# GpSimd's jump over the general path, the list building, the low halves and four weight loads, each moved within the rows' stage of a graph layer kernel

## The reference

```python
deg = jnp.maximum(jax.ops.segment_sum(jnp.ones(dst.shape), dst, 6250), 1.0)
xn = _layernorm(x)
# gnn: mean over the incoming edges, two linear layers
agg = jax.ops.segment_sum(xn[src], dst, 6250)
gnn = xn @ W1.T + b1 + (agg / deg[:, None]) @ W2.T + b2
# mix: linear attention, 16 heads of 32, relu on q and k
vk = einsum('bnhc,bnhd->bhcd', v_pad, k); vk_q = einsum('bnhd,bhcd->bnhc', q, vk)
mix = (vk_q[..., :-1] / (vk_q[..., -1:] + 1e-15)) @ proj_weight.T + proj_bias
x = x + gnn + mix
# ffn on layernorm(x): attention pooling -> gates -> two best of 8 experts, gelu, gelu
x = x + ffn(_layernorm(x))
```

## Time and profile before

| | us |
|---|---|
| three runs | 1461.55, 1464.06, 1466.59; median 1464.06 |
| the profiled execution | 1465.09 |
| its span, first to last instruction | 1462.9 |
| mean granted clock of TensorE | 0.977 of full |
| busy: PE / DVE / POOL / ACT | 1372.7 / 940.4 / 834.0 / 610.3 |

### The profile page before, as it was taken

The page is one execution under the profiler, slowest core; times in us unless marked ns, Lnnn a source line. Parts: engine busy times, 40 slices in busy tenths (PEclk is TensorE's granted clock), DMA queues, the critical chain, the costliest instruction groups (busy, mean ns, idle before and its releaser), DMA issues.

```text
span 1462.9 us, 22936 instructions
## 1 busy us (share of the span) xinstructions
PE 1372.7 (94%) x7764; PEld 625.1 (43%) x7764; DVE 940.4 (64%) x2087; ACT 610.3 (42%) x938; POOL 834.0 (57%) x907
## 2 busy tenths in 40 slices
PE   7888989999999999999999999899996889999997
PEld 3444434444444444444444444344442344444443
DVE  8877343222566877777777767666764466776677
ACT  5645223232233444444434444333332436555554
POOL 4653777777777777777777777777777200000000
PEclk9999999999999999999999999999998989999998
DMA  6854889998888888888887777877877341223322
GB/s 202 259 184 166 254 224 245 238 253 236 269 276 262 280 273 272 281 270 280 252 247 237 238 250 236 251 239 234 249 239 239 110 145 49 91 90 115 115 86 100
DMA packets 141205, 312.09 MB, mean 213 GB/s; under 512 B 40050, under 2 KB 42636, under 8 KB 141108
## 3 DMA queue, kind: packets, MB, share of 16 engines
q0 software_dynamic: 62560, 205.05, 46.7%
q1 hardware_dynamic: 62608, 77.26, 16.9%
q10 hardware_dynamic: 15940, 28.54, 5.3%
HBM read 260.53 MB, written 45.52 MB: 209 GB/s over the span
## 4 chain that ended last, share of the span: by engine, by line
PE 50%; POOL 25%; issue 10%; DVE 8%; DMA 4%; ACT 2%; SPq 0%; DVEq 0%; ACTq 0%; POOLq 0%
POOL ring L811 24%; PE bank L857 13%; PE bank L858 12%; PE bank L862 12%; PE bank L928 4%; DMA ring<-table,src_col 2%; PE bank L946 1%; PE bank L947 1%; PE bank L1121 1%; PE bank L996 1%; DVE xT L1669 1%; PE bank L997 1%; PE bank L998 1%; DVE st L1659 1%; DVE ring L2290 1%
## 5 line engine op out<-in xcount | busy, mean ns | idle before, releaser
L811 POOL DMA_INDIRECT ring<-table,src_col x782 | 759.6, 971 | 251.1 <-issue 242.7
L857 PE MATMUL bank<-wts,xT 128*128 128x512 f16 x588 | 226.2, 385 | 3.9 <-DVE wts L1875 2.1
L858 PE MATMUL bank<-wts,xT 128*128 128x512 f16 x588 | 226.0, 384 | 0.0
L928 PE MATMUL bank<-ring,hot 128*32 128x512 f16 x1560 | 121.3, 389 | 40.2 <-DMA ring<-table,src_col 32.1
L857 PE MATMUL bank<-wts,work 128*128 128x512 f16 x392 | 152.5, 389 | 1.5 <-ACT work L1463 1.4
L862 PE MATMUL bank<-wts,xT 128*128 128x512 f16 x588 | 152.9, 383 | 0.0
L858 PE MATMUL bank<-wts,work 128*128 128x512 f16 x392 | 151.6, 387 | 0.0
L1351 ACT ACTIVATE work<-bank,rd 128x512 f32<-128x512 f32 x49 | 33.7, 687 | 187.4 <-DVE rd L1832 186.3
L1899 DVE TENSOR_TENSOR work<-work 128x512 f16<-128x512 f32 x32 | 22.3, 696 | 137.6 <-ACT work L1409 137.4
L862 PE MATMUL bank<-wts,work 128*128 128x512 f16 x392 | 101.1, 380 | 0.0
L1593 ACT ACTIVATE work<-work 128x512 f32<-128x512 f32 x98 | 61.8, 630 | 79.9 <-DVE work L2300 78.8
(11 more groups left out here) (307 smaller groups left out, 2523.8 us busy)
## 6 DMA issues: line engine op xcount, KB each, us to landing
x_rows<-work ACTq DMA_DIRECT2D x51, 256.0 KB
ring<-table,src_col POOLq DMA_INDIRECT x782
work<-in_x ACTq DMA_DIRECT2D x48, 256.0 KB
ring<-x_rows SPq DMA_DIRECT2D x12, 1024.0 KB, 5.1
out_x<-ring SPq DMA_DIRECT2D x12, 1024.0 KB
table<-xT SPq DMA_DIRECT2D x45, 256.0 KB, 3.2
ring<-in_x SPq DMA_DIRECT2D x44, 256.0 KB, 3.3
spilled<-work SPq DMA_DIRECT2D x25, 256.0 KB, 3.8
```

What stands on the lines that cost most here:

```text
L811: pool.indirect_dma_start(ring[:, k, :], None, table[:, :], bass.IndirectOffsetOnAxis(ap=ap, axis=0)).then_inc(sem, 16)
L857: mm(out_, wh(c), mh(c), start=first and c == 0, stop=False)
L858: mm(out_, wh(c), ml(c), start=False, stop=False)
L928: r = mm(ps_unit[a:a + WIDE, :], hot[:, u % 2, DEEP * j + k, :], ring[:, slot(n, j), h * D:(h + 1) * D], start=(k == 0 and h == 0), stop=( ...
```

## The change

Six edits, all in the hand-written order:

1. POOL reads the flag at i = LISTS + 2 = 14, and jumps right behind its last high half; the waits for the last four row stores now stand behind the jump.
2. `judge_lists` signals `lists_made` by itself, and `place_units` and `make_lists` move to i = KP = 16, behind the last pair. POOL waits for the finished lists before the gathers of step 3 (`RG - 1`), which overwrite the scratch in `ring`.
3. From pair 5 on DVE makes the low halves of the pair before, behind the rates and moments of the present one.
4. On SP the V load stands before the store of row tile 42 and the Q load before that of tile 44; W1 and W2 move into the K stage, at i = FIRST + 2 and FIRST + 4.
5. FIRST is 18 and no longer 19: on PE, ACT and DVE the jumps and the first step come an iteration earlier, and the transposes by DMA begin with tile 20.
6. K_AT is 7.0 and no longer 5.0.

```diff
-FIRST = 19
+FIRST = 18
+BEHIND = 4
-K_AT, K_STEP, ... = 5.0, 5.75, ...
+K_AT, K_STEP, ... = 7.0, 5.75, ...
@@ SP @@
+                if r == T - XI + 1:
+                    weight(WV, qkv_w[2 * D:3 * D])
+                if r == T - XI + 3:
+                    weight(WQ, qkv_w[0:D])
                 n = TAIL if r == T - 1 else P
...
-            weight(WV, qkv_w[2 * D:3 * D])
-            weight(WQ, qkv_w[0:D])
             small()
...
-            sp.wait_ge(s["steps_act"], EDGES_ALL)
-            weight(G1, gw1)
-            weight(G2, gw2)
...
+                if i == FIRST + 2:
+                    sp.wait_ge(s["steps_act"], EDGES_ALL)
+                    weight(G1, gw1)
+                if i == FIRST + 4:
+                    weight(G2, gw2)
@@ POOL @@
-            pool.wait_ge(s["lists_made"], 1)
-            pool.wait_ge(s["steps_act"], ORDER.index(("src", 1)) + 1)
-            many = slow_tiles(pool)
-            for t in range(T - NS, T):
-                stored(pool, t)
+                if i == LISTS + 2:
+                    pool.wait_ge(s["lists_made"], 1)
+                    pool.wait_ge(s["steps_act"], ORDER.index(("src", 1)) + 1)
+                    many = slow_tiles(pool)
+            def table_stored():
+                for t in range(T - NS, T):
+                    stored(pool, t)
...
             with pool.If(many > 0):
+                table_stored()
+                pool.wait_ge(s["lists_made"], 2)
...
+            table_stored()
             for n in range(STEPS_END):
+                if n == RG - 1:
+                    pool.wait_ge(s["lists_made"], 2)
@@ DVE @@
                 link(V.tensor_scalar(slow_i[:], slow[:, 3:4], float(T), None, ALU.mult))
+                dve.sem_inc(s["lists_made"], 1)
...
                     moments(q)
-                    lows(q)
+                    if q < BEHIND:
+                        lows(q)
+                    if q > BEHIND:
+                        lows(q - 1)
+                    if q == PAIRS:
+                        lows(q)
...
-                if i == LISTS + 1:
+                if i == KP:
                     place_units()
-                if i == LISTS + 2:
                     make_lists()
```

More of the change, by code:

```diff
@@ L99 @@
 SEQ = [*range(38), LATE[0], *range(38, 42), LATE[1], *range(42, T - 2)]
-K_AT, K_STEP, M_PARTS, LAYER, GATHERS, LANDING, ADDING, UNITING = 5.0, 5.75, (7.5, 3.5, 8.0), 11.9, 5.02, 5.0, 0.55, 1.6
+K_AT, K_STEP, M_PARTS, LAYER, GATHERS, LANDING, ADDING, UNITING = 7.0, 5.75, (7.5, 3.5, 8.0), 11.9, 5.02, 5.0, 0.55, 1.6
 TURN = {t: i for i, t in enumerate(SEQ)}
```

## The result

| | before | changed |
|---|---|---|
| median of 20 runs each, us | 1463.78 | 1467.79 |
| ratio, 95% interval | | 1.0027 [1.0016, 1.0039] |
| profiled execution, us (span) | 1465.09 (1462.9) | 1465.87 (1464.0) |

The account below looks back on a forecast made before the run. The prediction took POOL's gather stream, through its start, as the bound: 8 us from the rows, 0 from the jump, 0 from the rest, so 1457.1 against the profiled 1465.09, 1456 us as median; range 1450.5 to 1462.

Parts of the forecast that it names:

- The start of the gathers sets the end: POOL issues gathers without a real pause, so what their start gains, the end gains, while PE keeps some idle time.
- They cost nothing at the end: FIRST and K_AT: about 10 us more PE waits for gathers in the K stage, costing 0 at the end.
- PE's later idle time as a store that holds waits: PE's 15.3 us idle from 700 to 1100 us and 11.5 us of waits after 1100 would absorb earlier PE waits.
- PE becomes the bound: Rival: PE delayed over 19 us by waits at the first steps; 1470 us at 25 us delay; chance one in fourteen.
- 8 us for the last row: Last row store before the gathers lands 8 us earlier, near 132.4 us, taken between bounds of 4 and 13 us.
- The stalls of PE were to be halved: Four PE stalls before the last row store, 9.57 us together, about half of each staying.
- V and Q loads at nothing: Loads moved ahead of the stores of tiles 42 and 44 cost nothing; without cover the last row lands up to 4 us later.
- The jump at 0: Moving POOL's jump ahead of the store waits gains 0; the 6.25 us gap belongs to the first indirect DMA.
- The rival had 3.25 us: Rival: the gap before the first gather is the jump's, gaining 3.25 us more, 1453 us; chance a quarter.
- First gather under 1 us behind the last landing: Sign at the start of the gathers that the forecast was wrong on the jump; it expected 6.3 us behind.
- POOL waiting more than 10 us for PE: Sign in POOL's waits for PE that the forecast was wrong on the bound; 8.4 us before the change.
- gathers earlier by more than the end: Sign that the forecast was wrong on the bound: the gathers gain more time than the end of the kernel does.

## Why the prediction was wrong, point by point

- **The start of the gathers sets the end.** Right as a rule, within 5 us, where there is no such stall: an earlier start of 5.8, 11.3, 11.6, 12.4, 12.8 and 12.9 us gave 4, 13.6, 12, 17, 16 and 14.6 us at the end (by the ratios). Two runs fall out of it: 8.8 us gave 5 with the low halves in their own turn, and 17.2 gave 9.5 with the weights where they stood, the two with the slower gathers.
- **"They cost nothing at the end"** (FIRST and K_AT). This is the step that failed. I costed the new plan by how late PE would meet the first gathers, and that was about right: 15.6 us of such waits between 141 and 350 us, so 7.7 more than the 7.9 of the earlier trace rows where I expected 10, and a first one of 5.73 us where I had 11. But I did not go through the new table for what each engine does between two neighbouring steps, though it was there to read. The term taken as 0 was about +16 us: 1450.88 with the old plan against 1467.79.
- **PE's later idle time as a store that holds waits.** Wrong as used. Idle time covers a wait only if it stands behind it *and* POOL is not held meanwhile. The ring is four steps deep; when PE stalls with POOL full, the gathers stop, and a gather not issued is never made up, since POOL issues without a pause ever after. PE's 15.3 us didn't shrink (20.7 us idle from 700 to 1100, from the row below); they changed their cause.

```profile
700.00:1100.00 400.00, 379.32 (x2266) 170.64 (x2265) 276.34 (x676) 156.59 (x239) 289.97 (x302) 0.99 0.78 238
```

- **The rival "PE becomes the bound".** Nearest to what happened, with the wrong place and mechanism: I looked for lateness in the K stage with a threshold of 19 us, and it was two waits of 4 to 5 us in layers 31 and 32, and what followed them. Part of it was true: the new plan left PE 18 us behind the gathers at step 131, near the 20 us that the ring allows, where it had been 14.
- **8 us for the last row.** The number is right, 8.75 us, in part by luck: the lists, costed at 4.2 us, brought 1.1; the low halves brought 7.3 to 8.9; and the loads, costed at nothing, took 1.4 back. The stalls of PE were to be halved; the four were 9.57 us, and what is left of them is 4.28 us. The two at the lists are gone, the comparison of first nodes has even grown:

```profile
80.16 0.91 PE L885 MATMUL bank<-wts,ones 128*128 128x128 f32 x6 [3.54 <-POOL wts L778]
...
115.12 0.62 PE L997 MATMUL bank<-ident,xT 128*128 128x128 f16 x8 [0.74 <-ACT xT L1381]
```

- **V and Q loads at nothing.** Wrong by a little: they hold up the last store by up to 1.4 us, not by the 4 us I named for the case that the cover is gone. In the time no difference was told apart.
- **The jump at 0.** Wrong. The gap went when flag and jump moved: 0.94 us is left, and the start gained 5.5 us more than the rows. The rival had 3.25 us, from DVE's 0.60 us as the nearest row. Started early, it was over before the landing: in the changed kernel the branch ends at 125.38, ahead of the last high half, POOL comes to the wait for the stores at 130.49, and the last one lands at 131.68. By the Trainium skill, Runtime: NRT & Kernel Launch, section Instruction fetch mechanics, a taken branch with its target outside the window waits for a DMA fetch; the packet of instructions in the gap agrees. The Trainium skill's GPSIMD Engine Reference, section Instruction dispatch, has the 6 us on a first call; here the first indirect DMA stood 0.94 us behind the store it waited for.
- **The signs named.** "First gather under 1 us behind the last landing" and "POOL waiting more than 10 us for PE" and "gathers earlier by more than the end": all three came.

## What to carry to other kernels

When a change moves work in a planned order, go through the new table for each resource that is handed back and forth (here one PSUM bank), and ask what the engine that frees it has queued ahead of freeing it; a planner that prices engines but not such hand-overs can lose by one place what the other edits win. Ask also how far the consumer is already behind: here a wait of 4 us was free while the ring had room, and was paid in full, with what followed it, once it had none. With the shared bank freed at an earlier place in the freeing engine's order, three plans of this kernel came within 1.3 us of each other. To weigh an edit in a stage whose absolute times scatter, compare distances between its own instructions. And idle time of an engine later in the program pays for a stall only if nothing upstream, like a stream of gathers with a ring of slots, stands still meanwhile.

## What the hardware showed that was not expected

- A jump of GpSimd over its general path, behind the last wait, held the first gather up by 3.01 us with the DMA engines 19% busy, and by 6.25 and 6.69 us in two traces with them 98% and 94% busy; one packet of instructions was fetched in each gap. Started some 6 us before the store landed, it left 0.94 us between landing and gather.
- Two waits of TensorE of 4.65 and 4.21 us cost the gathers 17.5 us, and three of 12.5 us in sum cost 21 us, with TensorE already 18 us behind the gathers; the matmuls at half clock behind each wait (0.92 and 0.91 of the clock over 20 us each) and waits of about 1 us in the layers that follow add to it. A wait of 4.27 us with TensorE 14.2 us behind cost nothing.
- The same wait of TensorE, 3.55 and 3.56 us for the compared first nodes, was followed by a stretch at the lower clock in one trace (0.77 over 15 us) and by none in another (1.00), and the rows came 2.9 us later with it.
